# Cross-attention and feed-forward block on one core: the fifth key tile holds the context twice, and V's context loads are issued from another queue

## The reference

```
def _L0_xattn_ref(latents, context, Wq, Wk, Wv, Wo):
    H, KV, HD = (16, 4, 96)
    hidden = jnp.concatenate([context, latents], axis=1)
    q = (latents @ Wq.T)
    k = (hidden @ Wk.T)
    v = (hidden @ Wv.T)
    ...
    scores = jnp.einsum('bkgqd,bksd->bkgqs', q, k) * scale
    attn = jax.nn.softmax(scores.astype(jnp.float32), axis=-1).astype(q.dtype)
    out = jnp.einsum('bkgqs,bksd->bkgqd', attn, v)
    ...
    return out @ Wo.T

x = x + _L0_xattn_ref(_layernorm(x, axis=-1), ctx_4096, Wq, Wk, Wv, Wo)
x = x + _L0_ffn_ref(_layernorm(x, axis=-1), ...)
```

## Time and profile before

| | us |
|---|---|
| median of 3 runs | 2206.69 (2204.3 to 2208.6) |
| the profiled execution's own time | 2205.26 |
| its span from first to last instruction | 2203.5 |
| PE busy in the span | 2157.3 (98%) |
| DVE, ACT, POOL busy | 768.9, 655.4, 696.5 |
| mean granted clock of PE | 0.996 |

### The profile page before, as it was taken

One profiled execution on the slowest core, in us unless ns is written; L12 is line 12 of the kernel. 1 busy time (PEld: TensorE's weight loads), 2 busy tenths in 40 slices (PEclk: granted clock), 3 DMA queues, 4 the chain that ended last, 5 costly groups with the idle time before them and its releaser, 6 DMA issues.

```text
span 2203.5 us, 30284 instructions
## 1 busy us (share of the span) xinstructions
PE 2157.3 (98%) x9948; PEld 1776.8 (81%) x9948; DVE 768.9 (35%) x1341; ACT 655.4 (30%) x1121; POOL 696.5 (32%) x565
## 2 busy tenths in 40 slices
PE   7999999999999999999999999999999999999998
PEld 6788888887777777778888878788887878888886
DVE  4223222167666666661110223222211132222222
ACT  3011111146666566662111222212123321111111
POOL 3500000136666666664212424100004422222221
PEclk9999999999999999999999999999999999999999
DMA  5632322535455554443433525311213532222222
GB/s 169 213 124 104 124 95 87 160 86 132 121 145 132 135 140 128 122 120 118 148 134 111 184 97 175 129 62 71 92 66 120 180 116 86 86 86 86 86 86 72
DMA packets 228028, 260.45 MB, mean 118 GB/s; under 512 B 73584, under 2 KB 141424, under 8 KB 227824
## 3 DMA queue, kind: packets, MB, share of 16 engines
q1 hardware_dynamic: 171696, 176.91, 25.4%
q10 hardware_dynamic: 56256, 82.57, 13.1%
HBM read 167.28 MB, written 91.88 MB: 118 GB/s over the span
## 4 chain that ended last, share of the span: by engine, by line
PE 86%; DMA 5%; DVE 3%; POOL 2%; issue 2%; ACT 2%; ACTq 0%; SPq 0%; DVEq 0%; POOLq 0%
PE psum L116 27%; PE psum L117 27%; PE psum L118 27%; PE psum L800 3%; DMA staging<-in_up_w 2%; PE psum L190 1%; POOL operands L1056 1%; ACT operands L1051 1%; DVE operands L972 1%; DVE small L951 1%; DMA staging<-in_x 0%; DMA staging<-in_wqkv 0%; DMA k_lo_scratch<-staging 0%; ACT psum L878 0%; DMA staging<-fold_scratch 0%
## 5 line engine op out<-in xcount | busy, mean ns | idle before, releaser
L116 PE MATMUL psum<-operands 128*128 128x512 f32 (+2 forms) x3016 | 1178.7, 391 | 24.7 <-DVE operands L304 12.0
L117 PE MATMUL psum<-operands 128*128 128x512 f32 (+2 forms) x3016 | 1162.7, 386 | 0.0
L118 PE MATMUL psum<-operands 128*128 128x512 f32 (+2 forms) x3016 | 1161.3, 385 | 0.0
L116 PEld LDWEIGHTS psum<-operands 128*128 128x128 f32 x3016 | 568.8, 189 | 139.5 <-DVE operands L304 12.0
L118 PEld LDWEIGHTS psum<-operands 128*128 128x128 f32 x3016 | 568.7, 189 | 112.2
L117 PEld LDWEIGHTS psum<-operands 128*128 128x128 f32 x3016 | 570.2, 189 | 96.9
L729 POOL TENSOR_TENSOR operands<-staging,operands 128x512 fp32r<-128x512 f32 x192 | 247.4, 1291 | 188.2 <-ACT operands L887 188.2
L951 DVE TENSOR_REDUCE small<-psum 128x1 f32<-128x576 f32 x256 | 193.4, 755 | 152.4 <-PE psum L800 152.4
L1056 POOL TENSOR_TENSOR operands<-staging,operands 128x512 fp32r<-128x512 f32 x92 | 118.3, 1296 | 368.1 <-ACT operands L1051 367.7
L1627 POOL TENSOR_TENSOR operands<-operands 128x640 fp32r<-128x640 f32 x64 | 100.0, 1566 | 325.5 <-ACT operands L1622 325.1
L1507 DVE TENSOR_TENSOR staging<-staging 128x512 f32<-128x512 f32 x64 | 45.9, 737 | 304.2 <-ACT staging L1473 303.4
(11 more groups left out here) (84 smaller groups left out, 1033.7 us busy)
## 6 DMA issues: line engine op xcount, KB each, us to landing
h_scratch<-staging ACTq DMA_DIRECT2D x80, 256.0 KB, 2.1
operands<-h_scratch SPq DMA_DIRECT2D x64, 320.0 KB, 3.1
operands<-recip_scratch SPq DMA_DIRECT2D x64, 192.0 KB, 3.1
o_scratch<-staging SPq DMA_DIRECT2D x64, 192.0 KB, 3.4
operands<-o_scratch SPq DMA_DIRECT2D x64, 192.0 KB, 2.6
operands<-q_hi_scratch ACTq DMA_DIRECT2D x14, 768.0 KB, 6.0
operands<-q_lo_scratch ACTq DMA_DIRECT2D x14, 768.0 KB, 6.5
staging<-in_wqkv SPq DMA_DIRECT2D x36, 256.0 KB, 3.4
```

Of the source, the lines that this page charges most:

```text
L116: e.matmul(o, lh, rh, start=first, stop=False)
L117: e.matmul(o, lh, rl, start=False, stop=False)
L118: return e.matmul(o, ll, rh, start=False, stop=last)
```

## The change

The fifth key tile gets the context's 64 keys twice. k's scratch rows are 640 columns wide instead of 576, and phase 0 stores the context's k twice, at columns 512 and 576 (12 transfers instead of 6). The scores of the fifth tile then hold the same exponentials in rows 0 to 63 and 64 to 127. V's fifth tile is stacked: the first operand has V's high part in rows 0 to 63 and its low part in rows 64 to 127; the second has the high part in rows 0 to 63 and zeros below. First operand × high exponentials gives both high × high and low × high; second × low exponentials gives high × low: two passes.

V's context rows are loaded by a new function, `b_load_vc`, with three transfers in place of two, issued by SP in the third head of a group; `b_load_v` on ACT keeps two of its four. POOL has 18 fills instead of 22.

```
-    k_d = [dram(f"k_{h}_scratch", (B * KVE, T)) for h in ("hi", "lo")]
+    k_d = [dram(f"k_{h}_scratch", (B * KVE, NT * P)) for h in ("hi", "lo")]
...
-                    e.dma_start(k_b[i][c * P:(c + 1) * P, :, S:T],
-                                raw(c_stage[c][i]).rearrange("p (b s) -> p b s", b=B)).then_inc(c_st, 16)
+                    for s0 in (S, T):
+                        e.dma_start(k_b[i][c * P:(c + 1) * P, :, s0:s0 + C],
+                                    raw(c_stage[c][i]).rearrange("p (b s) -> p b s", b=B)).then_inc(c_st, 16)
...
-            e.dma_start(raw(kp[p][i][0:HD, 0:T]), k_d[i][bass.ds(g * HD, HD), :]).then_inc(b_qk[p][i], 16)
+            e.dma_start(raw(kp[p][i][0:HD, :]), k_d[i][bass.ds(g * HD, HD), :]).then_inc(b_qk[p][i], 16)
...
-                e.dma_start(raw(vp[p][i][0:C, ST, 0:HD]), v_d[i][bass.ds(g * T + S, C), :]).then_inc(b_vl[p], 16)
+
+        def b_load_vc(e, g, p):
+
+            for i, to in ((0, vp[p][0][0:C]), (1, vp[p][0][C:P]), (0, vp[p][1][0:C])):
+                e.dma_start(raw(to[:, ST, 0:HD]), v_d[i][bass.ds(g * T + S, C), :]).then_inc(b_vl[p], 16)
...
+                    if hh % G == 2 and not (last and hh >= G):
+                        g = i * 2 + hh // G
+                        e.wait_ge(*past(b_pt, g * (G * NT)))
+                        e.sem_inc(idle, 1)
+                        b_load_vc(e, g + 1, 1 - hh // G)
...
-                vh, vl = (t[:, j, :] for t in vp[p])
-                parts3(e, PS[:, 6, :], vh, vl, pt[j][0], pt[j][1], j == 0, j == NT - 1).then_inc(b_pt, 1)
+                v0, v1 = (t[:, j, :] for t in vp[p])
+                if j < ST:
+                    parts3(e, PS[:, 6, :], v0, v1, pt[j][0], pt[j][1], j == 0, False).then_inc(b_pt, 1)
+                else:
+                    e.matmul(PS[:, 6, :], v0, pt[j][0], start=False, stop=False)
+                    e.matmul(PS[:, 6, :], v1, pt[j][1], start=False, stop=True).then_inc(b_pt, 1)
```

More of the change, by code:

```diff
@@ L424, in a_sp @@
                     if (c, h) == (10, 0):
-                        e.wait_ge(*past(c_st, 16 * (2 * KC + 8)))
+                        e.wait_ge(*past(c_st, 16 * (4 * KC + 8)))
                         e.sem_inc(idle, 1)
@@ L698, in b_sp_eng @@
             b_load_v(e, 0, 0)
+            b_load_vc(e, 0, 0)
             a_store(e, B - 1, A_EV - 1)
@@ L758, in b_pool @@
             for p in range(2):
[L759 to L763, removed]
+                fill(e, p * 3, kp[p][0][HD:HD + 1, :], 1.0)
+                fill(e, p * 3 + 1, kp[p][1][HD:HD + 1, :], 0.0)
+                fill(e, p * 3 + 2, qp[p][1][HD:HD + 1, :], 0.0)
             e.wait_ge(*past(a_acc, B * A_EV))
             for p in range(2):
[L766 to L771, removed]
+                fill(e, 6 + p * 6, vp[p][0][:, 0:ST, HD:VW], 1.0)
+                fill(e, 7 + p * 6, vp[p][0][0:C, ST, HD:VW], 1.0)
+                fill(e, 8 + p * 6, vp[p][0][C:P, ST, HD:VW], 0.0)
+                fill(e, 9 + p * 6, vp[p][1][:, 0:ST, HD:VW], 0.0)
+                fill(e, 10 + p * 6, vp[p][1][0:C, ST, HD:VW], 1.0)
+                fill(e, 11 + p * 6, vp[p][1][C:P, ST, :], 0.0)
             e.wait_ge(*past(b_cst, N_CST))
@@ L785, in b_pool @@
             scale(NI - 1, 2 * G - 1)
-        N_CST = 22
+        N_CST = 18
         def wo_part(i, q, off):
@@ L836, in pv @@
                     if a == 0:
-                        e.wait_ge(*past(b_vl[p], 64 * nth(i, o, 2 * G) + 64))
+                        e.wait_ge(*past(b_vl[p], 80 * nth(i, o, 2 * G) + 80))
                 if j % 2:
@@ L861, in b_pe @@
             e.wait_ge(*past(a_ev, B * A_EV - 2))
-            e.wait_ge(*past(b_cst, 10))
+            e.wait_ge(*past(b_cst, 6))
             b_pe_row(e, 0, 2)
```

## The result

| | before | after |
|---|---|---|
| median, four runs each | 2207.64 us (2204.3 to 2211.47) | 2183.61 us (2182.27 to 2184.98) |
| span of the profiled execution | 2203.5 | 2181.3 |

The ratio is 0.9892, with a 95% interval from 0.9878 to 0.9905. The profiled execution took 2183.1 us, against the forecast of 2183.0.

A forecast was written before the change was run, and what follows sets the result against it. It took what TensorE issues, plus about 26 us of waits on DVE's row maxima, to bound the attention. Terms −14.5 − 9.0 + 1.2 = −22.3 us against 2205.3 gave 2183.0 us, range 2178 to 2191.

The forecast's parts named there:

- The pass removed: Fifth tile of each attention head: one 512-column pass fewer on TensorE in 64 heads, 14.5 us saved, bounds 0 and 15.0.
- The sign to look for: Intervals of the row's transposition in the attention: 8.04 us where 8.27 stood, 8.1 to 8.2 where 8.99 and 8.59 stood.
- V's context loads leave ACT: Every fourth attention head: two of four load issues leave ACT, so a late exponential runs on time; 9.0 us saved.
- The residual of 0.11: Long attention heads: cost in us left for the two load issues remaining on ACT, allowed for ten heads.
- the 10.1 that I had counted: Extra us of all fifteen long attention heads together, each taken against 8.28, laid to ACT's issues of V's loads.
- SP takes three issues: Once in four heads: SP's three new loads delay the row's placement by 0.5 to 0.9 us, hidden by slack; cost 0.
- k with 640 columns and the fills: Attention's k load grows from 216 to 240 KB, landing in perhaps 6.4 us; POOL's fills drop to 18; cost 0.
- The start: Start of the kernel: six more stores of k on ACT delay SP and then PE, costing 1.2 us, between 0 and 5.0.
- The start at its upper bound: Rival: at the start, stores and weight loads share the DMA engines, costing 5 us or more; 2187 to 2189, chance 0.13.
- The pass saved off the clock: Rival: ACT's copy-out or DVE's maxima pace the attention heads, so the pass saves no time; 2197 or 2190, chance 0.12.
- The long heads stay: Rival: the loads remaining on ACT still come before the exponential, so V's long heads stay long; 2192, chance 0.06.
- SP holds the placement: Rival: SP's three issues hold the row's placement until PE waits at the next head's scores; slower, chance 0.02.

## Why the prediction was right

**The sum, −22.3.** The medians differ by 24.0 us and the two profiled spans by 22.2. That the forecast lies 0.1 us from the profiled execution is partly luck. In the spans, the 60 intervals gained 23.2 where the two terms had 23.5, what follows the last transposition gained 0.9, for which there was no term, and the start lost 1.9 where the term had 1.2. The executions of the kernel after alone differ by 2.7.

**The pass removed, −14.5.** Right: 0.2355 us a head, 14.1 over the 60 intervals. The 0.01 a head that I set aside for ACT's copy-out did not come. The sign to look for was in the 45 other heads, which went from 8.316 to 8.088 on average.

**V's context loads leave ACT, −9.0.** Right in size, 9.1 by the kernel with the third pass put back, and right in mechanism: the same gain came with the loads on ACT a head later. The move alone gave 7.6 in its one trace, with two long single heads in it. The residual of 0.11 for ten heads was not there: the long heads of the kernel after average 8.091, against 8.088 for the others. With the third pass put back, the fifteen long heads gave 9.5 of the 10.1 that I had counted, and the 45 others took 0.5 more than before. What I had not seen is how much hangs on the number of issues ahead of the exponential. The operand without the move has three context loads on ACT, five issues in all, and then nothing of the pass's gain was left. With four, the pass brought 10.2 and not 14.1 in one trace each, a difference that chance can make. One reading of mine was too strict: PE's loads also had waits without a releaser in the attention, 1.7 us in 11 cases, which changes nothing in the sum.

**SP takes three issues, 0.** Right, for the reason given, but the placement came 1.5 us later and not 0.5 to 0.9: three issues take 0.68 each with their gaps (654.31 to 656.34), 2.0 together, and SP had 0.9 of idle time. The slack held it.

**k with 640 columns and the fills, 0.** Right. The load of 240 KB lands in 6.3 us, where 216 KB took 6.1 and I had allowed 6.4:

```profile
operands<-k_hi_scratch ACTq DMA_DIRECT2D x14, 240.0 KB, 6.3
```

**The start, +1.2.** Not confirmed. The one profile after shows 1.9, but the doubled stores alone gave 1.0001, and the stalls of either kind of kernel overlap. What the doubled stores are worth lies between −2.4 and +2.7 us, so 1.2 is neither shown nor refuted. I had also put the stall on the stores and the weight loads. It goes away with the load of x that SP issued ahead of its first store. A share of the DMA engines above 1 spoke of no single culprit, and the order of SP's issues did. The Trainium skill (DMA: Bandwidth & Descriptors, Specifications) asks for 512 bytes a run, from which I had put the start nearer to 3 us; no run here shows that, and the interval ends at 2.7.

**The rivals.** The start at its upper bound (2187 to 2189): no, since the store-doubled kernel is as fast as before. The pass saved off the clock (2197 or 2190): no, the common heads are 8.04 to 8.07. The long heads stay (2192): no, 8.06. SP holds the placement: no, though it was held 1.5 us longer where I had said 0.5 to 0.9.

## What to carry to other kernels

Transfers issued by an engine that also computes cost their issue time, 0.4 to 0.6 us each, wherever an instruction that the bound engine needs stands behind them: put them where that engine is ahead, a head later on the same engine served as well as another queue. Count them before you add one: the pass removed with one issue more ahead of the exponential brought nothing. Measure the parts of a change apart and together, and before you explain what is missing in their sum, look whether it lies in single iterations and how much those vary between executions of the same code. And look at what was issued ahead of a late store: behind a load of 2 MB a store of 256 KB landed in 9 to 11 us instead of 4, and moving the load brought 8 to 10 us.

## What the runs showed of the hardware

A pass over 64 rows between passes over 128 is dearer than a full one: 0.41 and 0.43 us between starts where full passes had 0.31 and 0.24, and 0.64 us a head in all (523.48 − 485.34 over 60) against 0.2355 for the full pass of zeros. The weight loads then no longer run ahead, 0.25 us twice. The Trainium skill (TensorEngine Tiling (Array Packing), Key Properties) says that a change of tiling mode drains TensorE. The gaps agree with that, though whether it is the height, the upper half as its place or the change between them was not tried apart. A change of height alone is not enough: a pass over 97 rows starts 0.23 behind one over 128 (658.21 to 658.44 in the rows of the full pass of zeros).

One issue of V's loads in each of the fourteen kernels, always in the group that stands at 574 to 591 us, takes 1.4 to 2.0 us where its like takes 0.5. In all fourteen an issue on SP's queue that starts within 0.8 us of it takes 1.1 to 1.6 us too (1.32 at 585.21 in the kernel before), so it is not ACT's queue alone. Why was not tried.
